# Four graph layers on one core: the last two attention heads in turns by groups of tiles, and the end of layer 3's products in another order

## The reference, cut to what matters

```python
def _L3_gnn_ref(x, edge_index, Ws, Wb, a_w, a_b):
    v_src, v_tgt = (edge_index[0], edge_index[1])
    n = x.shape[0]
    outs = []
    for h in range(Ws.shape[0]):
        Wx = x @ Ws[h] + Wb[h]
        d = Wx.shape[-1]
        s = Wx[v_tgt] @ a_w[h, :d] + Wx[v_src] @ a_w[h, d:] + a_b[h]
        s = jax.nn.leaky_relu(s, negative_slope=0.2)
        alpha = _segment_softmax(s, v_tgt, n)
        outs.append(jax.ops.segment_sum(alpha[:, None] * Wx[v_src], v_tgt, num_segments=n))
    return jnp.stack(outs, axis=1).reshape(n, -1)
...
x = _layernorm(x + _L3_gnn_ref(x, edge_index, L3_gnn_Ws, L3_gnn_Wb, L3_gnn_a_w, L3_gnn_a_b), axis=-1)
```

## Time and profile before

| | us |
|---|---|
| median of 3 runs | 421.08 (420.71 to 422.01) |
| profiled execution, its time | 420.92 |
| profiled execution, its span | 419.1 |
| TensorE busy | 384.1 (92%) |
| VectorE busy | 280.8 (67%) |
| ScalarE busy | 250.9 (60%) |
| GpSimd busy | 93.9 (22%) |

### The profile page before, as it was taken

How to read it: one execution, slowest core, us unless ns; L and a number is a source line. 1 busy time by engine, 2 the same in 40 slices (tenths; PEclk the granted TensorE clock), 3 DMA queues, 4 the chain that set the end, 5 groups by cost and what they waited for, 6 DMA issues and landing times. The chain is left out here.

```text
span 419.1 us, 8557 instructions
## 1 busy us (share of the span) xinstructions
PE 384.1 (92%) x2908; PEld 229.4 (55%) x2908; DVE 280.8 (67%) x608; ACT 250.9 (60%) x406; POOL 93.9 (22%) x86
## 2 busy tenths in 40 slices
PE   1799889999999999999999999999997999999950
PEld 1344438544444444544444544455555889999950
DVE  7778999739985774235533223553896878999883
ACT  9779777485622367613644310367665999998125
POOL 4510000049900375103724000233000000121210
PEclk9999998999999999999999999999999999999995
DMA  5940006005000000000000000000003022210005
GB/s 195 388 133 2 1 1 202 2 0 203 0 0 2 0 0 2 0 2 1 2 0 2 0 0 2 0 2 0 2 2 103 20 82 82 73 53 2 4 3 203
DMA packets 10041, 18.53 MB, mean 44 GB/s; under 512 B 2129, under 2 KB 2321, under 8 KB 10001
## 3 DMA queue, kind: packets, MB, share of 16 engines
q1 hardware_dynamic: 9136, 14.86, 10.3%
q10 hardware_dynamic: 864, 3.15, 2.1%
HBM read 15.87 MB, written 2.13 MB: 43 GB/s over the span
## 5 line engine op out<-in xcount | busy, mean ns | idle before, releaser
L710 PE MATMUL ps<-big,xTs 128*128 128x512 f16 x384 | 86.2, 379 | 1.6 <-ACT xTs L435 1.5
L710 PEld LDWEIGHTS ps<-big,xTs 128*128 128x128 f16 (+1 forms) x384 | 36.6, 98 | 43.4 <-issue 1.8
L637 ACT ACTIVATE big<-big,uvt 128x1024 bf16<-128x1024 f32 x55 | 58.6, 1138 | 0.0
L407 POOL TENSOR_TENSOR big<-xcur,big x24 | 27.7, 1155 | 128.5 <-ACT xcur L528 128.5
L527 ACT ACTIVATE big<-xcur,nmr,rstd (+1 forms) x24 | 19.5, 813 | 37.8 <-DVE nmr L1313 37.8
L435 ACT ACTIVATE big<-ps 128x512 f16<-128x512 f32 (+2 forms) x25 | 14.5, 579 | 42.7 <-PE ps L710 32.7
L743 PE MATMUL ps<-big,xTs 128*128 128x512 f32 x64 | 35.6, 653 | 0.0
L1323 DVE SCALAR_TENSOR_TENSOR big<-ps,big 128x512 f32 (+1 forms) x16 | 11.0, 690 | 31.0 <-ACT big L435 31.0
L418 POOL TENSOR_TENSOR xcur<-xcur,c 128x512 f32<-128x512 f32 x7 | 8.3, 1183 | 103.1 <-DVE c L1521 103.1
L1007 PE MATMUL ps<-big,cst 128*128 128x260 f16 x256 | 29.7, 275 | 0.0
L1207 DVE TENSOR_TENSOR c<-c,ps 128x80 f32 (+31 forms) x64 | 23.2, 362 | 9.7 <-PE ps L764 6.6
(11 more groups left out here) (205 smaller groups left out, 688.1 us busy)
## 6 DMA issues: line engine op xcount, KB each, us to landing
big<-u_rows ACTq DMA_DIRECT2D x6, 512.0 KB, 3.7
xTs<-in_xT SPq DMA_DIRECT2D x2, 1024.0 KB, 9.2
xcur<-in_x SPq DMA_DIRECT2D x1, 2048.0 KB, 17.8
out<-xcur SPq DMA_DIRECT2D x8, 256.0 KB, 2.1
big<-in_W SPq DMA_DIRECT2D x1, 1024.0 KB, 5.9
cts<-in_W3T SPq DMA_DIRECT2D x1, 1024.0 KB, 13.2
xTs<-in_W1T SPq DMA_DIRECT2D x1, 1024.0 KB, 5.4
xTs<-in_wc SPq DMA_DIRECT2D x1, 1024.0 KB, 8.3
```

The lines of the kernel that those rows point to most:

```text
L407: pool.tensor_tensor(cur[:, 1, 1, t, :], xcur[:, t, :], cur[:, 1, 0, t, :], ALU.subtract).then_inc(S["x_lo"], 1)
L637: act.activation(above[:, a % AHEAD, :], uf[:, h % 2], ACT.Relu, scale=BIG, bias=vb[:, j, h:h + 1]).then_inc(S["above_in"], 1)
L710: return mm(bank, lhs(k)[a], rhs(k)[b], start=start and k == 0 and n == 0, stop=stop and k == KT - 1 and n == 2)
```

## The change

Two parts, in one diff.

- The tail. Heads 6 and 7 (`PAIR` is 6) are computed in turns by group: (6, b0), (7, b0), (6, b1), (7, b1), (6, b2), (7, b2), with banks 2 and 3, 4 and 5, 6 and 7. ScalarE scales them group by group. `last_sum(b)` on VectorE combines and adds both heads of a group at once; `combine_scaled` and GpSimd's addition of head 6 are gone. The statistics are split into heads 0 to 4, 5, and 6 with 7. `last_scales(b - 1)` stands inside `last_sum(b)`. Norms of tiles 2, 5 and 7 are VectorE's, of 0, 1, 3, 4 and 6 ScalarE's.
- The end of layer 3. `y_lower` of tiles 5 and 6 is GpSimd's, with a semaphore of its own (`y_lo_pool`), for which `exps(7)` and TensorE's j = 5 and 6 wait. VectorE does `wx_evict(7)` and `y_whole(7)` right behind `y_whole(6)`, then the limits, then `y_lower(7)`, then the flag. The transpose of `lim` stands behind j = 3 instead of j = 1. `score_bias` moves ahead of the scales of the last tile's norm in layer 2.

```diff
-STAT_COLS = (0, 5 * DH, 7 * DH, D)
+PAIR = H - 2
+STAT_COLS = (0, 5 * DH, PAIR * DH, D)
+NORM_ACT, NORM_DVE = (0, 1, 3, 4, 6), (2, 5, 7)
...
+            for t in (NT - 3, NT - 2):
+                pool.wait_ge(S["y_hi"], t + 1)
+                pool.tensor_tensor(yh[:, t, 1], yf[:, t % 2].rearrange("p h e d -> p h (e d)"), yh[:, t, 0],
+                                   ALU.subtract).then_inc(S["y_lo_pool"], 1)
...
-                for h in range(H - 1):
+                for h in range(PAIR):
                     pool.wait_ge(S["att_in"], h + 1)
...
-                act.wait_ge(S["y_lo"], t + 1)
+                if isinstance(t, int) and t == NT - 1:
+                    act.wait_ge(S["y_lo_pool"], 1)
+                else:
+                    act.wait_ge(S["y_lo"], t + 1)
...
+                for b in range(2):
+                    scaled_sums(PAIR, b)
+                    scaled_sums(PAIR + 1, b)
+                deviations(0)
+                scaled_sums(PAIR, 2)
+                last_norms(0)
+                scaled_sums(PAIR + 1, 2)
+                deviations(1)
+                last_norms(1)
+                deviations(2)
+                last_norms(2)
...
+                if j == 3:
                     pe.wait_ge(S["lim_in"], 1)
                     pe.transpose(ps[0:1, 3, P:2 * P], lim[:, 3:4], id32[:]).then_inc(S["lim_done"], 1)
...
+                for b, (t0, t1) in enumerate(LAST_BANKS):
+                    for h in (PAIR, PAIR + 1):
+                        if b == 0:
+                            pe.wait_ge(S["cz_ready"], (h + 1) * NT)
+                        pe.wait_ge(S["comb_ready"], 2 * (PAIR - 1) if b == 0 else 2 * PAIR)
+                        for t in range(t0, t1):
+                            ins = head_tile(h, t)
+                        ins.then_inc(S["head_done"], 1)
...
+            def score_bias(t, i):
+                dve.wait_ge(S["wa_done"], 2)
+                tt(crow[:, 0:1], ps[0:H, 3, 256:257], abc[:], ALU.add).then_inc(S["crow_r"], 1)
+                tt(crowb[:], ps[:, 3, 264:264 + H], abb[:], ALU.add).then_inc(S["crow_r"], 1)
+            norm_loop(2, total2, score_bias)
...
-            dve.memset(qc[:, :, NT:OS], 1.0).then_inc(S["qz"], 1)
...
+            link(dve.memset(qc[:, :, NT:OS], 1.0))
...
+                    dve.wait_ge(S["head_done"], PAIR + 2 * b + 2)
+                    dve.wait_ge(S["scaled"], 2 * t1)
+                    link(tt(c, c, o[:, :, :, DH + 1:YW], ALU.subtract))
+                    link(tt(c, c, dense[:, t0:t1, PAIR:H, :].rearrange("p t h d -> p h t d"), ALU.add))
+                    if b > 0:
+                        last_scales(b - 1)
+                    link(dve.reciprocal(rdf[:, :, t0:t1], c[:, :, :, DH]))
+                    part = c[:, :, :, 0:DH]
+                    link(tt(part, part, rdf[:, :, t0:t1].unsqueeze(3).broadcast_to([P, 2, n, DH]), ALU.mult))
+                    xs = xcur[:, t0:t1, PAIR * DH:D].rearrange("p t (h d) -> p h t d", h=2)
+                    link(tt(xs, xs, part, ALU.add))
```

More of the change, by code:

```diff
@@ L642, in _, with scaled_sums @@
                         next_row(h - 1)
-                h = H - 2
-                act.wait_ge(S["head_done"], h + 1)
-                act.wait_ge(S["x_added"], h - 1)
-                for t in range(NT):
-                    scaled_sum(h, t)
-                h = H - 1
-                act.wait_ge(S["x_added"], h - 1)
-                for b, (t0, t1) in enumerate(LAST_BANKS):
-                    act.wait_ge(S["head_done"], H + b)
-                    for t in range(t0, t1):
+                def scaled_sums(h, b):
+                    act.wait_ge(S["head_done"], PAIR + 2 * b + (h - PAIR) + 1)
+                    if b == 0:
+                        act.wait_ge(S["x_added"], h - 1)
+                    for t in range(*LAST_BANKS[b]):
@@ L664, in u_copy @@
+                act.wait_ge(S["y_lo_pool"], 2)
                 def u_copy(h, q):
@@ L693, in _ @@
                 act.wait_ge(S["scale8"], 1)
-                for t in range(NT - 1):
+                for t in NORM_ACT:
                     act.activation(xcur[:, t, :], xcur[:, t, :], ACT.Identity, bias=nmr[:, t:t + 1], scale=rstd[:, t:t + 1]).then_inc(S["out_act"], 1)
@@ L1057, in head, with head_tile @@
                     for t in range(NT):
-                        o = ps[:, 2 + 3 * q + t // 3, t % 3 * YW:(t % 3 + 1) * YW]
-                        for j in range(NT):
-                            for v in range(2):
-                                ins = mm(o, cz[h % CZ][:, j, t * P:(t + 1) * P], yh[:, j, v, h, :],
-                                         start=j == 0 and v == 0, stop=j == NT - 1 and v == 1)
-                        if t == NT - 1 or h == H - 1 and t % 3 == 2:
-                            ins.then_inc(S["head_done"], 1)
-                for h in range(H):
-                    head(h)
+                        ins = head_tile(h, t)
+                    ins.then_inc(S["head_done"], 1)
+                def head_tile(h, t):
+                    bank = 2 + 3 * (h % 2) + t // 3 if h < PAIR else 2 + 2 * (t // 3) + h - PAIR
+                    o = ps[:, bank, t % 3 * YW:(t % 3 + 1) * YW]
+                    for j in range(NT):
+                        for v in range(2):
+                            ins = mm(o, cz[h % CZ][:, j, t * P:(t + 1) * P], yh[:, j, v, h, :],
+                                     start=j == 0 and v == 0, stop=j == NT - 1 and v == 1)
+                    return ins
+                for h in range(PAIR):
+                    head(h)
+                for b, (t0, t1) in enumerate(LAST_BANKS):
+                    for h in (PAIR, PAIR + 1):
+                        if b == 0:
+                            pe.wait_ge(S["cz_ready"], (h + 1) * NT)
+                        pe.wait_ge(S["comb_ready"], 2 * (PAIR - 1) if b == 0 else 2 * PAIR)
+                        for t in range(t0, t1):
+                            ins = head_tile(h, t)
+                        ins.then_inc(S["head_done"], 1)
             with pe.Else():
@@ L1449, in _ @@
             y_whole(0, 0)
-            with dve.Fori(0, NT // 2 - 1) as r:
+            with dve.Fori(0, NT // 2 - 2) as r:
                 for i in (1, 0):
@@ L1455, in _ @@
                     y_lower(t - 1, 1 - i)
+            wx_evict(NT - 3, 1)
+            y_whole(NT - 3, 1)
+            y_lower(NT - 4, 0)
+            wx_evict(NT - 2, 0)
+            y_whole(NT - 2, 0)
             wx_evict(NT - 1, 1)
-            y_lower(NT - 2, 0)
+            y_whole(NT - 1, 1)
             dve.wait_ge(S["uc_in"], NT)
@@ L1465, in _ @@
             stt(lim[:, 3:4], lim[:, 1:2], VMAX * BIG, lim[:, 3:4], ALU.is_le, ALU.mult).then_inc(S["lim_in"], 1)
-            y_whole(NT - 1, 1)
+            y_lower(NT - 1, 1)
             dve.wait_ge(S["lim_done"], 1)
@@ L1469, in _ @@
             dve.tensor_copy(flags[:, 2:3], lim[0:1, 1:2]).then_inc(S["mode"], 1)
-            y_lower(NT - 1, 1)
             before_branch = links[0]
@@ L1503, in combine_open @@
                     tt(c, c, o[:, :, :, DH + 1:YW], ALU.subtract).then_inc(S["comb_ready"], 1)
-                def combine_scaled(h):
-                    o = sums(h)
-                    c = comb[:, h % 2].rearrange("p (a b) d -> p a b d", a=3)
-                    dve.wait_ge(S["head_done"], h + 1)
-                    dve.wait_ge(S["scaled"], NT)
-                    tt(c, c, o[:, :, :, DH + 1:YW], ALU.subtract).then_inc(S["comb_ready"], 2)
                 def combine_close(h):
```

77 lines of the change are left out of this document (35 added, 42 removed).

## The result

| | before | after |
|---|---|---|
| median of 4 runs each, side by side | 421.40 us (420.71 to 422.01) | 415.30 us (415.07 to 416.21) |
| ratio, 95% interval | | 0.9862 (0.9845 to 0.9878) |
| profiled execution, its time | 420.92 | 415.07 |
| profiled execution, its span | 419.1 | 413.3 |
| last norms begin | 414.92 | 408.99 |

The kernel is 1.4% faster: 5.8 us between the two profiled executions, where the prediction said 4.4. The 415.3 us lies in its range. I use four places in the program to say where the time went: the flag in the middle of layer 2 (the reduction into `f_flag`, at some 132 us), the first `uc` (at 292 us), the addition that closes head 5, and the start of the last norms.

The account below looks back on a forecast made before the run. Bound: TensorE's heads up to 396.9 us, then VectorE's combining, statistics and norms. The tail's 4.9 us less 0.5 at the end of layer 3 gave 4.4 off the span and a 416.7 us median, range 414.4 to 418.4.

Parts of the forecast that it names:

- The tail: From closing head 5 to the last norms: VectorE alone counts, and the last norms begin at 410.0 instead of 414.92, 4.9 us less.
- The price of an element: VectorE's combining in the tail: 1.04 ns each, so 0.56 us for a pair of heads over three tiles, 0.43 for two.
- the rival in which the pair costs more than its elements: Tail: the groups' four operations at half rate cost 6.2 us more, giving 422.9 us; chance 0.05.
- The cover of the last scaling: Tail: ScalarE's scalings of (7, b2), behind norms 0 and 1, are done some 0.7 us before VectorE wants them.
- most of where the gain comes from: Tail: VectorE's wait through ScalarE's six norms, two chains of 2.22 us, was said to give most of the 4.9 us.
- `score_bias`: Start of layer 3's tail: moved into VectorE's wait for the last deviation, it saves 0.2 us for all that follows.
- `y_whole` behind GpSimd: End of layer 3: `y_whole(6)` and `y_whole(7)` stand until GpSimd's subtraction ends and finish 1.1 us later.
- an operation whose data lie in SBUF stood: Reading of two earlier rows: such VectorE operations stood until GpSimd was through, while `combine` operations reading PSUM did not stretch.
- The free overlap: Rival, end of layer 3: `y_whole` does not wait for GpSimd, 1.3 and 0.2 us are kept, 414.8 us; chance 0.13.
- The end of layer 3: TensorE's early partial sums end at 324.65 against 323.93 because of waits for GpSimd: 0.7 us more, 0.5 with `score_bias`.
- The flag's lateness: End of layer 3: the flag comes at 322.7 instead of 319.63, ScalarE's first eviction 1.1 us later, back at 0.5 by 339.
- The rival in which it is carried into the heads: ScalarE's 1.1 us is not made up, or GpSimd takes longer: 417.3 to 418.3; chance 0.20 together with the thin cover.

Follow-up runs that it names:

- e9_scales_earlier: The kernel before with only last_scales(b - 1) put inside last_sum(b), heads still one after the other: 419.02 us, ratio to before 0.9939.
- e6_norms_on_act: The changed kernel with the last norms of tiles 0 to 6 on ScalarE and only 7 on VectorE: 415.90 us, ratio to before 0.9864.
- e2_layer3_only: The kernel before with only the end of layer 3 and `score_bias` changed, the tail as before: 420.67 us, ratio to before 0.9978.
- e7_written_out: The kernel before with only tiles 5 and 6 of layer 3 written out behind VectorE's loop, same order: 420.26 us, ratio to before 0.9966.
- e4_held: The changed kernel with GpSimd's subtractions held back until `y_whole(6)` and the limits, respectively, are done: 415.06 us, ratio to before 0.9845.
- e5_halves: The changed kernel with each of GpSimd's two subtractions cut into two of four heads each: 414.50 us, ratio to before 0.9826.

## Why the prediction was right, and where it was off

- **The tail, 4.9 predicted, 5.14 measured.** Right step by step, in the sum and in the mechanism: VectorE's chain without a stand. Head 5's closing to the first group: 5.8 predicted, 5.75 measured; the first group 3.7 and 3.75; the second with scales 3.95 and 4.01; the last with scales 3.15 and 3.16; the last scales 0.4 and 0.39. What was over-priced are the two norms on VectorE, 0.55 and 0.5 for 0.39 and 0.45: the price came from the last norm's whole duration, where a next instruction begins before the one ahead of it is over. The price of an element held: 390 of them took 0.56 and 260 took 0.42, so the rival in which the pair costs more than its elements is out. The cover of the last scaling was 0.7 predicted and 0.88 measured.
- **What the gain is made of.** The sentence that "most of where the gain comes from" is the wait through ScalarE's norms was too strong. VectorE stood 0.28 us for the first of the two chains and 2.48 for the second, 2.76 us or about half of the 5.14. The order that shortens that wait brings 1.8 us by itself (e9_scales_earlier), and handing two norms to VectorE, 0.1 (e6_norms_on_act).
- **`score_bias`, 0.2 predicted, 0.34 measured.** The two tiny additions were priced by ScalarE's 0.22 us wait; two kernels with it (after and e2_layer3_only) agree on 0.34 and 0.33 from `f_flag` to the first `uc`, so the term was mis-sized.
- **`y_whole` behind GpSimd.** Right: the 1.1 us behind GpSimd's end was 1.08 both times, and 1040 elements took 2.15 and 2.16 for 2.17. The two rows at 113 and 401 us, whose shorter operations ended 0.03 and 0.22 us behind GpSimd, give the standing; the size of 1.1 is not in them, and the prediction doesn't work it out. The Trainium skill's page "SBUF — State Buffer", section "Who interferes with whom", says that a VectorE instruction with two SBUF inputs and a GpSimd instruction that reads SBUF contend for a port pair that is an exclusive lock, so that the one that comes second blocks; every row here of such a pair agrees, in both directions. The reading "an operation whose data lie in SBUF stood" was too wide: a reduction of `cnt` at 112.99 us, with one operand from SBUF, took 0.16 us beside GpSimd. The `tensor_scalar` at 113.19 has one operand too and stood all the same; no run here says why. The free overlap, which I gave 0.13, did not happen.
- **The end of layer 3, +0.7 predicted, +0.30 measured.** The step that failed is one that I did not make: the diff moves tiles 5 and 6 out of VectorE's loop, and I took them for the same work. Written out they cost 0.53 us less (e7_written_out), 0.21 of it ahead of GpSimd's first subtraction, which sets the pace here: it and all behind it start 0.2 to 0.3 us sooner than I had them. Some 0.15 more is the second transpose: I let the last 32 matmuls begin 0.32 us behind `lim_in`, by the transpose's length of 0.27, and they begin 0.11 behind its start (319.33 against 319.22), as in the kernel before. The rest of the chain (1.54 and 1.11 us of waits, 32 matmuls in 3.81 us for 3.76) came as written.
- **The flag's lateness is absorbed.** Right. In after's own frame, ScalarE's first eviction is 1.4 us later than before (31.71 against 30.32 from the first `uc`; 1.1 predicted: from the flag to this eviction it takes 2.26 us, and the prediction allowed 1.9). Its eviction at 338.05 is 0.30 us later than the one at 338.84 before, so by then it has caught up, as the prediction said (339), and at 343.53 ScalarE stands 0.24 us for TensorE. In e4_held and e5_halves the flag moved by +0.12 and -1.95 us and the end by -0.68 and -1.31, each time TensorE's number within 0.02. The rival in which it is carried into the heads is out.
- **The total.** 4.4 predicted; 5.1 for the change between the profiles: 0.24 from the tail, 0.4 from the end of layer 3 and 0.14 from `score_bias`, less 0.1 behind the norms. The remaining 0.75 of the 5.8 us arose ahead of the change, most of it at 20 us. So of the 1.4 us between 4.4 and 5.8, one half comes from terms that were mis-sized, nearly all in the same direction, and the other half belongs to the two executions.

The change is right as a whole, though one half of its second part works against it: without GpSimd, the new order at the end of layer 3 would have brought 2.3 us more.
